# Transposing quantised activations by DMA in place of TensorE and ScalarE, in a decoder layer on one core

## The reference

```python
def act_quant(x):
    scale = 127.0 / jnp.clip(jnp.max(jnp.abs(x), axis=-1, keepdims=True), EPS)
    q = jnp.clip(jnp.round(x * scale), -128.0, 127.0) / scale
    return x + jax.lax.stop_gradient(q - x)
...
def h_bitlinear(x, w):
    xq = act_quant(fwht(x))
    wq = weight_quant(w)
    return jnp.einsum('bsh,oh->bso', xq, wq)
gate = h_bitlinear(hidden_states, w_gate)
up = h_bitlinear(hidden_states, w_up)
return h_bitlinear(jax.nn.silu(gate) * up, w_down)
```

## Time and profile before

| | us |
|---|---|
| median of 3 runs | 1811.16 (1810.85 to 1812.78) |
| profiled execution, its own time | 1813.1 |
| span of the profiled execution | 1811.3 |
| PE busy | 1626.2 (90%) |
| PE weight loads busy | 1002.6 (55%) |
| DVE busy | 1380.3 (76%) |
| ACT busy | 826.8 (46%) |
| POOL busy | 184.3 (10%) |
| DMA, share of 16 engines, queue of SP | 23.1% |
| mean granted TensorE clock | 0.964 of full speed |

### The profile page before, as it was taken

How to read it: one execution, slowest core, us unless ns; L and a number is a source line. 1 busy time by engine, 2 the same in 40 slices (tenths; PEclk the granted TensorE clock), 3 DMA queues, 4 the chain that set the end, 5 groups by cost and what they waited for, 6 DMA issues and landing times.

```text
span 1811.3 us, 25396 instructions
## 1 busy us (share of the span) xinstructions
PE 1626.2 (90%) x10470; PEld 1002.6 (55%) x10470; DVE 1380.3 (76%) x1759; ACT 826.8 (46%) x784; POOL 184.3 (10%) x154
## 2 busy tenths in 40 slices
...
DMA packets 100122, 75.73 MB, mean 42 GB/s; under 512 B 6044, under 2 KB 85148, under 8 KB 99496
## 3 DMA queue, kind: packets, MB, share of 16 engines
q1 hardware_dynamic: 100008, 74.10, 23.1%
...
## 4 chain that ended last, share of the span: by engine, by line
PE 78%; DVE 9%; ACT 8%; issue 2%; DMA 1%; POOL 1%; SPq 1%; POOLq 0%; ACTq 0%; DVEq 0%
PE psum L508 12%; PE psum L658 11%; PE psum L596 7%; PE psum L609 6%; PE psum L685 6%; PE psum L702 6%; PE psum L532 6%; PE psum L554 6%; PE psum L575 5%; ACT ffn_mem L733 3%; PE psum L638 2%; PE psum L694 2%; DVE ffn_mem L1086 2%; PE psum L677 1%; PE psum L542 1%
## 5 line engine op out<-in xcount | busy, mean ns | idle before, releaser
L733 ACT ACTIVATE ffn_mem<-psum 128x1024 f32<-128x1024 f32 x160 | 159.9, 1021 | 390.4 <-PE psum L630 148.7
L1013 DVE TENSOR_REDUCE mneg<-psum 128x4 f32<-128x1024 f32 x256 | 306.5, 1219 | 37.7 <-PE psum L575 34.4
L736 ACT ACTIVATE attn_mem<-psum 128x1024 f32<-128x1024 f32 x256 | 249.4, 1019 | 87.2 <-PE psum L609 85.0
L575 PE MATMUL psum<-kst,attn_mem 96*128 96x256 bf16 x1024 | 149.4, 277 | 25.2 <-DMA attn_mem<-q_dram 8.7
L609 PE MATMUL psum<-attn_mem,kst 98*128 98x512 bf16 x512 | 148.1, 391 | 21.2 <-ACT attn_mem L736 10.7
L1144 POOL TENSOR_TENSOR grstd<-gvare,neg_half 128x1 f32<-128x1 f32 x32 | 17.6, 551 | 1353.6 <-DVE gvare L912 1353.6
L1105 DVE TENSOR_TENSOR ffn_mem<-ffn_mem 128x1024 f32<-128x1024 f32 x128 | 150.8, 1219 | 1.2
L685 PE MATMUL psum<-had,ffn_mem 128*128 128x128 f32 x1024 | 127.2, 277 | 22.2 <-ACT ffn_mem L733 22.2
L596 PE MATMUL psum<-attn_mem,vpad 128*32 128x256 f32 x2048 | 138.1, 394 | 2.5 <-ACT attn_mem L736 2.5
L575 PEld LDWEIGHTS psum<-kst,attn_mem 96*128 96x128 bf16 x1024 | 96.1, 99 | 76.1 <-issue 20.7
L824 ACT ACTIVATE ffn_mem<-psum,sc 128x1024 f32<-128x1024 f32 x64 | 69.7, 1114 | 148.2 <-PE psum L658 148.0
...
## 6 DMA issues: line engine op xcount, KB each, us to landing
attn_mem<-q_dram SPq DMA_DIRECT2D x192, 128.0 KB, 7.7
...
x_in<-in_x SPq DMA_DIRECT2D x16, 512.0 KB, 3.8
...
c_in<-in_ctx SPq DMA_DIRECT2D x16, 128.0 KB, 2.2
```

Source lines behind the costliest of these rows:

```text
L575: last = mm(region(f"max{u}")[:, i * T:(i + 1) * T], qst[0:KR, GQ * g + i, t * P:(t + 1) * P], kst[0:KR, g, :], start=True, stop=True)
L733: return nc.scalar.activation(dst, src, ACT.Copy)
L736: return nc.scalar.activation(dst, src, ACT.Exp, **kw)
L1013: nc.vector.tensor_reduce(mneg[:, h, t, GQ * g:GQ * (g + 1)], region(f"max{u}").rearrange("p (h t) -> p h t", h=GQ), AX_X, ALU.max, negate ...
```

## The change

The three transposes of quantised integers (`d_qx` for both tiles, `c_q` for t = 0 and t = 1) are taken off PE and ACT. SP issues them as DMA transposes instead, from SBUF to SBUF: two of 128 x 512 for `d_qx`, one of 128 x 2048 for each `c_q`. The PSUM slots of these units go, and so do their ACT copies. `qdT` gets one buffer for each t. To make room, `r3` lies in the first half of `act_f`; DVE therefore waits, before the butterflies of t = 1, until both stores of the batch before are done. A constant of ones moves to another buffer. All five order lists are written anew.

```diff
-        qdT = sb("qdT", [P, FC, P], BF16)
-        r3 = sb("r3", [P, LT, D])
-        ones = r3[:, 0, 0:P]
+        qdT = sb("qdT", [P, LT, FC, P], BF16)
+        r3 = act_f[:, 0:8, :].rearrange("p (l c) t -> p l (c t)", l=LT)
+        ones = upper[:, P:L]
...
-            "sp": """t_load.2-3 t_load.0-2 x_fetch-1 x_split-2 x_stack.0-2 t_load.1-2 x_stack.1-2 s_mT.0-2 s_mT.1-2 c_store.0-3
-                c_store.1-3""",
+            "sp": """s_mT.0-2 x_stack.1-2 t_load.1-2 c_q.0-3 s_mT.1-2 t_load.2-2 t_load.0-1 c_q.1-3 x_fetch x_split-1 x_stack.0-1
+                c_store.0-3 c_store.1-3 d_qx-2""",
...
+                def d_qx(self, n):
+
+                    after(sp, qx_made, n)
+                    for t in range(LT):
+                        sp.dma_start_transpose(qxT[:, :, t * P:(t + 1) * P], qx[:, t, :]).then_inc(qxT_in.sem, 16)
+
+                def c_q(self, n, t):
+
+                    after(sp, qd_made, n, t + 1)
+                    if n:
+                        unit_filled(sp, f"dn{t}", n - 1)
+                    sp.dma_start_transpose(qdT[:, t], qd[:, :]).then_inc(qdT_in[t].sem, 16)
...
-                def d_qx(self, n):
-                    fill_begins(pe, "qxT", n)
-                    after(pe, qx_made, n)
-                    o = region("qxT").bitcast(BF16)[:, 0:1024].rearrange("p (c l) -> p c l", c=DC)
-                    for c in range(DC):
-                        for t in range(LT):
-                            last = tr(o[:, c, t * P:(t + 1) * P], qx[:, t, c * P:(c + 1) * P], ident16[:, :])
-                    fill_ends(last, "qxT")
...
                 def c_gate(self, n, j):
                     if j == 0:
-                        after(pe, qxT_made, n)
+                        after(pe, qxT_in, n)
...
-                def c_q(self, n, t):
-                    u = f"q{t}"
-                    fill_begins(pe, u, n)
-                    after(pe, qd_made, n, t + 1)
-                    for c in range(FC):
-                        last = tr(region(u).bitcast(BF16)[:, c * P:(c + 1) * P], qd[:, c * P:(c + 1) * P], ident16[:, :])
-                    fill_ends(last, u)
...
                 def c_dn(self, n, t):
...
-                    after(pe, qdT_made, n, t + 1)
+                    after(pe, qdT_in[t], n)
...
-                def d_qx(self, n):
-                    unit_filled(act, "qxT", n)
-                    copy(qxT, region("qxT").bitcast(BF16)[:, 0:1024].rearrange("p (c l) -> p c l", c=DC))\
-                        .then_inc(qxT_made.sem, 1)
...
-                def c_q(self, n, t):
-                    u = f"q{t}"
-                    unit_filled(act, u, n)
-                    copy(qdT[:, :, :].rearrange("p c t -> p (c t)"), region(u).bitcast(BF16)).then_inc(qdT_made.sem, 1)
...
                 def c_fly(self, n, t, s):
 
                     if s == 0:
+                        if t == 1:
+                            after(dve, stored[0], n - 1)
+                            after(dve, stored[1], n - 1)
...
                 def c_qd(self, n, t):
                     after(dve, hd_round, n, t + 1)
                     if t:
-                        after(dve, qdT_made, n, t)
+                        after(dve, qdT_in[0], n)
```

More of the change, by code:

```diff
@@ L157, in decoder_layer @@
         lower = [act_f[:, 8 * i:8 * i + 8, :].rearrange("p c t -> p (c t)").bitcast(BF16) for i in range(2)]
[L158 removed]
+        tern = [qd[:, :], qdT[:, 0].rearrange("p c t -> p (c t)")]
         orders = {
[L161 to L192 removed]
@@ new lines, in decoder_layer @@
+            "act": """t_quarter.1.2-3 t_quarter.1.3-3 x_q1-2 t_quarter.2.0-3 x_kst.0-2 t_quarter.2.1-3 t_quarter.2.2-3 t_quarter.2.3-3
+                x_k.1-1 d_hT-3 d_hx-3 x_q.3-1 d_round-3 c_gate.0-3 c_gate.1-3 s_mT.0-2 c_gate.2-3 t_quarter.0.0-2 c_gate.3-3
+                t_quarter.0.1-2 x_kst.1-2 s_scores.0-2 c_dT.0.0-3 t_quarter.0.2-2 c_dT.0.1-3 c_H.0.0-3 c_H.0.1-3 s_scores.1-2
+                s_scores.2-2 c_dT.1.0-3 c_dT.1.1-3 c_round.0-3 s_scores.3-2 c_H.1.0-3 c_H.1.1-3 t_quarter.0.3-2 s_scores.4-2
+                s_scores.5-2 s_mT.1-2 s_scores.6-2 s_scores.7-2 x_split-1 c_round.1-3 t_quarter.1.0-2 s_scores.8-2 s_scores.9-2
+                s_scores.10-2 t_quarter.1.1-2 s_scores.11-2 s_scores.12-2 s_scores.13-2 s_scores.14-2 s_scores.15-2 x_load""",
@@ new lines, in decoder_layer @@
+            "dve": """x_q2-2 t_abs.2-3 t_sum.2-3 s_out.1-3 d_ln-3 t_quarter.2.0-3 t_lower.2.1-3 t_quarter.2.1-3 t_lower.2.3-3
+                t_quarter.2.2-3 t_quarter.2.3-3 d_norm-3 d_had-3 t_abs.0-2 x_k.1-1 t_sum.0-2 s_max.0-2 t_lower.0.1-2 s_max.1-2
+                s_max.2-2 d_hx-3 s_max.3-2 x_q.3-1 d_qx-3 t_quarter.0.0-2 s_max.4-2 s_max.5-2 t_quarter.0.1-2 s_max.6-2
+                s_max.7-2 x_v.1-1 c_up.0-3 t_quarter.0.2-2 s_mT.0-2 t_lower.0.3-2 t_quarter.0.3-2 c_up.1-3 c_fly.0.0-3 x_ctx-1
+                c_fly.0.1-3 c_up.2-3 c_fly.0.2-3 c_up.3-3 c_fly.0.3-3 c_fly.1.0-3 x_o.1-1 c_fly.1.1-3 s_max.8-2 c_fly.1.2-3
+                s_max.9-2 c_fly.1.3-3 c_H.0.1-3 s_max.10-2 s_max.11-2 c_qd.0-3 s_max.12-2 s_max.13-2 t_abs.1-2 t_sum.1-2
+                s_pv.0-2 s_max.14-2 s_max.15-2 s_pv.1-2 x_norm-1 t_lower.1.1-2 s_mT.1-2 t_quarter.1.0-2 c_H.1.1-3 x_split-1
+                t_quarter.1.1-2 s_pv.2-2 t_lower.1.3-2 c_qd.1-3 t_quarter.1.2-2 t_quarter.1.3-2 c_dn.0-3 s_pv.3-2 s_pv.4-2
+                s_pv.5-2 s_out.0-2 c_norm.0-3 c_dn.1-3 s_pv.6-2 s_pv.7-2 c_norm.1-3""",
@@ L193, in decoder_layer @@
+            "pool": """t_lower.1.0-3 t_lower.1.2-3 s_copy-2 t_lower.2.0-3 t_lower.2.2-3 d_ln-3 t_lower.0.0-2 t_lower.0.2-2 x_prep-1
+                x_o.1-1 c_dn.0-3 c_dn.1-3""",
         }
```

57 lines of the change are left out of this document (27 added, 30 removed).

## The result

The changed kernel is slower. Its median is 1837.33 us (1833.62 to 1838.05, 4 runs), that of the kernel before, on the same chip, 1811.97; the ratio is 1.0136, with a 95% interval of 1.0124 to 1.0149. The forecast was 1781, range 1762 to 1818. The profiled execution took 1833.62 us, the shortest of the four.

A forecast was written before the change was run, and what follows sets the result against it. PE's list was taken as the bound, period 101.1 us; less 2.3 removed and 0.3 from the new order, 98.5. From 1813.1 us, 14 periods give -36 and the end +3: 1780, stated as 1781, range 1762 to 1818.

The forecast's parts named there:

- So PE's list is the bound.: Kernel before, steady period: PE busy 97.3 of 101.0 us, with short waits where it meets DVE or ACT through PSUM slots.
- the waits of PE lie after `x_o`: New lists: PE's waits fall in the stretch behind x_o, 5.5 us there and 0.1 in the rest of the period.
- What is removed: Per batch, two c_q and eight d_qx pieces leave PE, 2.3 us; three copies leave ACT, 4.8 us; plain gain 32 us.
- The landing, taken as 5 and 4 us: DMA transposes on SP: issue to landing taken as 5 us for each c_q and 4 us for d_qx.
- All three are covered: PE work hides the landings: 8.5 and 6.0 us against 5 for c_q, 4.5 against 4 for d_qx.
- The new order: Walk of the new lists behind x_o: PE waits sum to 5.5 us, giving back 0.3 us; period 98.5.
- the walk's clock: Time scale of the forecast's walk through the new lists, with the end of x_o as 0.
- The sum: Whole kernel: 1813.1 us profiled, -36 steady, +3 at the end, giving 1780; stated as 1781.
- The +3 of start and end: Last batches: +1.5 for the last c_qd landing, +3 for d_qx, -2 for two c_q less on PE; nothing at the start.
- signs of being wrong: PE waiting over 1 us for a DMA each period, late s_mT.1, or DVE never idle while PE waits 8 us or more.
- (b): Rival, no change: DVE falls 2.5 us further behind between s_max.0 and s_mT.1, period 101 again, 1811 or above; 8%.
- (a): Rival, slower: transposes land late, 11.1 us for c_q and 6.4 for d_qx, +7.0 us a period, some 1930; 15%.

The follow-up runs named there:

- experiment 7: Experiment 1's kernel with DVE's statistics of y moved behind the last butterfly, as a separate step; 1781.56 us, ratio 0.9839 to the kernel before.
- experiment 9: Experiment 7's kernel with s_max.9 moved ahead of c_H.0.0 and s_max.10 between c_dT.0.1 and c_H.0.1 on PE; 1779.67 us, ratio 0.9821.
- experiment 1: The changed kernel with x_prep moved behind x_o and c_dn.0 in POOL's list; 1799.82 us, ratio 0.9928 to the kernel before.
- experiment 5: Experiment 1's kernel with each c_q transpose issued twice, the second after the first has landed; 1850.07 us, ratio 1.0213 to the kernel before.

## Why the prediction was wrong, step by step

- **"So PE's list is the bound."** Nearly so before, but not in the new lists: behind `x_o` the chain runs through DVE up to `s_max.8` and then between PE and ACT, and in experiments 7 and 9 through DVE alone, up to the slot of `c_H.1.1`. The prediction saw the place ("the waits of PE lie after `x_o`") and that DVE had less PE work beside it, and still summed PE's waits.
- **"What is removed", 2.3 us**, and ACT's copies: held. Where the clock stays up, PE is busy 94.7 us a period (experiment 1) where "near 95" was forecast.
- **The landing, taken as 5 and 4 us**: 4.3 and 2.5. "All three are covered": held; experiment 5 confirms the cover behind both `c_q`. SP holds a `c_q` for 1.9 us, so it is not late. By the Trainium skill's page "DMA: Bandwidth & Descriptors" the estimate was 4.0 us from its rate, close to the trace, and 3.4 us of SP from its cycles per tile, nearly twice the trace.
- **"The new order", waits of 5.5 us**: this is the step that failed. It walked the lists with each piece at the duration of a row of before, and priced the new order at 0.3 us a period gained; it lost 3.6. On the walk's clock, which starts at `s_scores.0`, `c_dT.1.0` was to start at 12.4. It started at 15.6, in the long periods at 16.9, and from there on nothing more was lost: `c_dn.0` came at 30.6 for 27.4, `c_dn.1` at 41.7 for 38.4. Three things were missing.
  - POOL's list was not walked, so `x_prep` beside the butterflies was not seen. The sum for y starts at 1.3, in experiment 1 at 0.2: 1.1 us. `c_dT.0.1`, due at 6.6, started at 7.8, in experiment 1 at 6.7.
  - The PE pieces behind the waits were priced at the upper clock. `c_H.0.1` takes 3.3 us for 2.0, so 1.3 more; in the four long periods `c_dT.0.1` takes 1.9 for 1.1 as well, 2.6 more in all. That is 1.7 on average.
  - `c_dT.1.0` was to wait for the last butterfly. It waits for a slot that an exponential empties behind two copies, and starts at 13.2 in experiment 1 with the clock up, 0.8 late; the period there is 99.52, 1.0 above the forecast.

  1.0 + 1.1 + 1.7 = 3.8 of the 3.93 us between 98.5 and 102.43. One error went the other way and is contained in these figures: the table of ACT was loaded before `x_o` ended, and `c_H.0.0` waited 0.83, not 2.2.
- **The sum.** Experiment 7, with a period of 98.62 and a median of 1781.56, meets the forecast of 98.5 and 1781 almost exactly, and that is luck. The order forecast was that of experiment 1, which has 99.52 with the clock up and 1799.82; experiment 7 has the statistics of y behind the butterflies, where the walk had them ahead. The +3 of start and end was luck too, as said above.

None of the prediction's signs of being wrong appeared: no wait of `c_dn` or of the first gate for a DMA in the steady part, no late `s_mT.1` because of SP, no 8 us of waits on PE beside a DVE without idle time. It failed in a way that it had no sign for. The clock's fall was in none of its terms or rivals.

Of the rivals, (b), "PE's list no longer binds", was the nearest, with 8%; it was priced at a standstill for a DVE that is 2.5 us late, or above. The sum for y came only 1.1 us late, and the time rose by 25 us. (a) did not occur. The range's upper bound, 1818, reached up through (b) and left out what a late DVE does to PE's clock. What stays open: why the clock falls in some periods and stays up in others behind the same waits (four and nine of 13 in experiment 1), and why the first mark comes 7.7 us later. Whether `x_prep` beside the butterflies alone, on the old lists, would cost the same was not tried; there it can't start so early.
